# A decoder layer on one core: the maximum of the cross attention's scores runs 15 steps ahead of the scores instead of 17

## The reference, cut to what matters

```python
x = layernorm(x + linear_attention(x))              # 8 heads of 64
Q = (x @ Wq + bq)    # 16 heads of 16, 2048 queries
K, V = (ctx @ Wk + bk), (ctx @ Wv + bv)             # 1601 keys
attn = softmax(Q K^T / sqrt(16), axis=-1)
x = layernorm(x + (attn @ V) @ Wo + bo)
x = layernorm(x + moe(x))    # 16 experts, the best 4 of each token, and a shared one
```

## Time and profile before

| | us |
|---|---|
| runs | 1095.07, 1096.03, 1097.78 |
| median | 1096.03 |
| profiled execution | 1086.56 |
| its span | 1084.7 |
| mean granted TensorE clock | 0.940 of full speed |
| TensorE busy | 951.4 (88%) |
| VectorE busy | 732.9 (68%) |
| ScalarE busy | 648.0 (60%) |

### The profile page before, as it was taken

How to read it: one execution, slowest core, us unless ns; L and a number is a source line. 1 busy time by engine, 2 the same in 40 slices (tenths; PEclk the granted TensorE clock), 3 DMA queues, 4 the chain that set the end, 5 groups by cost and what they waited for, 6 DMA issues and landing times.

```text
span 1084.7 us, 19088 instructions
## 1 busy us (share of the span) xinstructions
PE 951.4 (88%) x6868; PEld 521.9 (48%) x6868; DVE 732.9 (68%) x1171; ACT 648.0 (60%) x1403; POOL 254.6 (23%) x306
## 2 busy tenths in 40 slices
PE   6997998779999999999999999998990698988890
PEld 2454566334444444444444444443340586776670
DVE  0206886798999998989989899889120343324773
ACT  1322223118888887878878788777870265654560
POOL 1006113600000000200002000000465255773654
PEclk9999999859999999999999999999895799999996
DMA  9007892200322112112211010011642246554763
GB/s 346 8 1 179 101 129 92 94 5 2 100 81 86 42 50 84 37 35 58 86 55 27 8 27 22 25 53 50 142 148 75 86 142 137 158 157 148 242 214 131
DMA packets 75800, 99.29 MB, mean 92 GB/s; under 512 B 17566, under 2 KB 58784, under 8 KB 75390
## 3 DMA queue, kind: packets, MB, share of 16 engines
q1 hardware_dynamic: 64252, 73.73, 26.8%
q0 software_dynamic: 7584, 20.79, 5.4%
q10 hardware_dynamic: 3872, 3.56, 1.0%
HBM read 52.45 MB, written 43.35 MB: 88 GB/s over the span
## 4 chain that ended last, share of the span: by engine, by line
PE 60%; DVE 17%; DMA 8%; issue 7%; POOL 6%; ACT 2%; SPq 0%; POOLq 0%; DVEq 0%; ACTq 0%
PE psum L1163 16%; PE psum L1053 13%; DVE mpart L1466 9%; PE psum L1149 7%; PE psum L1318 6%; POOL sorted_d L677 4%; PE psum L982 3%; PE psum L1336 3%; PE psum L1015 3%; DMA x_in<-sorted_d 2%; DMA given_d<-y_out,x_in 2%; PE psum L1279 2%; DMA sorted_d<-x_rows,slots 2%; PE psum L1103 1%; PE psum L1187 1%
## 5 line engine op out<-in xcount | busy, mean ns | idle before, releaser
L937 ACT ACTIVATE region<-psum 128x512 f32<-128x512 f32 (+1 forms) x832 | 448.6, 610 | 132.0 <-PE psum L1149 117.6
L1466 DVE TENSOR_REDUCE mpart<-psum 128x2 f32<-128x1024 f32 x384 | 461.7, 1222 | 39.4 <-PE psum L1053 36.4
L1163 PE MATMUL psum<-region 128*32 128x256 f32 (+1 forms) x3120 | 251.8, 395 | 7.4 <-ACT numT L852 7.4
L1053 PE MATMUL psum<-kstack,qstack 63*128 63x512 f32 (+1 forms) x1024 | 223.0, 463 | 19.9 <-DVE mpart L1466 19.5
L1053 PEld LDWEIGHTS psum<-kstack,qstack 63*128 63x128 f32 x1024 | 92.9, 194 | 194.0 <-issue 123.7
L1149 PE MATMUL psum<-qstack,kstack 64*128 64x512 f32 (+1 forms) x832 | 176.1, 412 | 0.1
L1683 DVE SCALAR_TENSOR_TENSOR silu_h<-tanh_h,psum 128x128 f32<-128x128 f32 x110 | 31.6, 287 | 150.7 <-ACT tanh_h L907 149.4
L1149 PEld LDWEIGHTS psum<-qstack,kstack 64*128 64x128 f32 (+1 forms) x832 | 111.3, 184 | 17.6 <-ACT region L937 14.5
L1163 PEld LDWEIGHTS psum<-region 128*32 128x32 f32 (+1 forms) x3120 | 62.2, 108 | 118.1 <-issue 75.7
L1318 PE MATMUL psum<-w_all,xT_in 128*128 x376 | 103.3, 399 | 3.8 <-issue 1.7
L685 POOL DMA_INDIRECT given_d<-y_out,x_in x94 | 93.4, 994 | 44.8 <-ACT y_out L921 27.3
(11 more groups left out here) (172 smaller groups left out, 937.5 us busy)
## 6 DMA issues: line engine op xcount, KB each, us to landing
x_in<-sorted_d SPq DMA_DIRECT2D x94, 129.0 KB, 2.5
sorted_d<-x_in SPq DMA_DIRECT2D x7, 1548.0 KB, 7.3
given<-given_d SPq DMA_DIRECT2D x16, 512.0 KB, 4.6
qstack<-qparts_d SPq DMA_DIRECT2D x96, 64.0 KB, 2.3
kstack<-kparts_d SPq DMA_DIRECT2D x6, 800.5 KB
qparts_d<-region SPq DMA_DIRECT2D x4, 1024.0 KB, 4.1
kparts_d<-region SPq DMA_DIRECT2D x4, 800.5 KB, 10.1
xT<-in_xT SPq DMA_DIRECT2D x1, 2048.0 KB, 9.2
```

Of the source, the lines that this page charges most:

```text
L937: act.activation(prob[0:rows_of, s % 3, j, :], ring(n)[0:rows_of], ACT.Exp).then_inc(ring_read, 1)
L1053: mm = pe.matmul(bank(unit_bank(u) + side)[:, at * w:(at + 1) * w], qstack[rows_of, buffer(G), p, t * P:(t + 1) * P], kstack[rows_of, g * ...
L1163: mm = pe.matmul(bank(NUM_BANK)[VW * j:VW * (j + 1), q], vals[0:r, g, kt, j, :], prob[0:r, s % 3, j, q], start=(kt == 0 and half == 0), st ...
L1466: dve.tensor_reduce(mpart[:, G % 2, qt, :, p, n], both, X, ALU.max).then_inc(max_read, 1)
```

## The change

LEAD falls from 17 to 15 steps, so that 30 units instead of 34 lie ahead of step 0 (24 instead of 28 in the lead-in loop), each group's last unit falls into kt = 10 instead of kt = 8, and all units are done after step 192 instead of 190. SP's stack_max moves from kt = 9 to kt = 11.

```diff
-LEAD = KT + 4
+LEAD = KT + 2
 FIRST_UNIT_AT = TILES + 7
 UNITS_IN_LOOP = TILES + 13 - FIRST_UNIT_AT
-STACK_MAX_AT = 9
+STACK_MAX_AT = 11
```

## The result

The changed kernel is slower. On another chip, where both are 12 to 13 us faster, twelve runs gave 1090.85 against 1083.97, ratio 1.0061 (1.0042 to 1.0080). The forecast was 1103.4.

What follows compares the result with a forecast made beforehand. Bound: TensorE and VectorE, without slack, until the slots are ready at step 188, then GpSimd's scatter. Lead-in -2.5, boundaries +8.9, clock +1, elsewhere 0 make +7.4 on 1096.03: 1103.4 us, range 1097.5 to 1109.

Steps and rivals of the forecast that it cites:

- Part 1: Lead-in: with four units fewer ahead, step 0's score loads start earlier, limited by group 0's maximum landing; gain 2.5 us.
- Part 2: Group boundaries: the maximum comes two steps later, its DMA chain outlasts the room, and TensorE stalls; loss 8.9 us.
- The eight plain boundaries: Into groups 1, 2, 3, 4, 6, 8, 10, 12: chain 5.5 us against room 4.6, so 0.9 us stall each.
- The five with longer steps: Into groups 5, 7, 9, 11, 13: out projection or gate work widens the room to 5.7 us; 0.25 us each.
- Part 3: TensorE's granted clock during the steps: between none and two more falls than before; +1 us, bounds -1.5 and +6.
- rival (b): TensorE's clock falls at most group boundaries, adding 12 us to the stalls, 1114.4 us in all; chance 0.08.
- Part 4: Last steps, SP's order, expert loads and scatter: moved work is covered or unwaited for; 0 us, bounds -6.7 and +3.
- finish_max passes some short gate operations on VectorE: VectorE's queue: finish_max moves past gate operations before which its reads are ordered anyway; cost 0.
- Nobody waits for them: SP's queue: loads issued ahead of the later maximum go out in what was a wait, with no waiter; cost 0.
- slots ready 6 to 8 us after 758.9: Sign of being right: VectorE has the slots of chunks 0 to 2 ready (step 188) that much later than before.
- (a): Boundary stalls cost nothing, as TensorE makes them up or the chain fits; 1093.5 or 1092.0 us; chance 0.07.
- (c): With later loads the first scatter lands in 2.6 us instead of 9.36, giving the loss back; 1096.7 us; chance 0.08.

Runs made afterwards that it cites:

- half the reads: The changed kernel with VectorE reading only the first 256 of each 512 scores; a read took 0.69 us instead of 1.22, a plain step still 2.47 us.
- the longer chains: The changed kernel with one or two more DMAs (copies of max_d) between the write's landing and the four reads; ratios to the kernel before 1.0182 and 1.0443.

## Why the prediction was right, point by point

**Part 1, the lead-in.** Forecast 2.5 us, measured 2.3 to 2.6 (237.3 and 236.8 against 239.6 and 239.4). The reason is shown: the first scores wait for the DMA, and with two reads instead of four they come 1.2 us earlier still.

**Part 2, the boundaries.** Forecast 8.9 us, measured 9.5 and 8.5. In the first profile two inner sizes were off, in ways that cancel. The eight plain boundaries cost 1.13 each instead of 0.95, the chain having a mean of 5.7 over these eight (5.3 to 6.1) where SP's mean wait had given 5.5. One mean hides two kinds: four chains with a quick landing and four with a slow one. The estimate by the Trainium skill had 1.3 for each of the eight.

The Trainium skill, "DMA: Bandwidth & Descriptors", section "Anatomy of one DMA", gives its 2.0 us for DMAs that GpSimd issues. Those here are issued by SyncE, and the quick landing of the write took 1.4 us, the slow ones 1.9 to 2.2.

The five with longer steps cost 0.09 instead of 0.25. Where each would and wouldn't wait was right at all fourteen. What the prediction had wrong is that nothing comes back: 0.12 us does in the step behind each stall, 1.2 in all. TensorE is at its own rate in a plain step, as half the reads show, but the first half step after a stall runs a little shorter.

**Part 3, the clock.** Forecast +1 us, and this step failed, harmlessly. No fall of the clock was added. In the first profile the one of before came again; after the start of the steps the clock rose sooner (the first three steps take 7.8 and 9.1 us in its two profiles, 9.4 and 10.1 in those of before), which gives 1.0 to 1.6 in these pairs. So the size was of the wrong sign here. That the change is the reason isn't shown: over all profiles these three steps take 8.3 to 10.1 at lead 17 and 7.1 to 9.2 at lead 15. The mechanism that the term stood for, rival (b), is real and begins just beyond this change: with the chain 0.6 us longer it is already half of what is lost on top.

**Part 4, elsewhere.** Forecast 0 with bounds of -6.7 and +3. The step that failed is "finish_max passes some short gate operations on VectorE", costed at 0. What is moved past the gate's work is not finish_max alone but the two short units ahead of it as well, and whole units that take their place cost 0.7 us in each of two groups, 1.4 in all; the other way round, step 0 of groups 8 and 12 (2.78 before) loses its delay behind the gate's work, 0.6 in all beyond the 0.12. The four units at the end and the last boundary's wait, though the last wait was up to 6.4 us and not 2, changed nothing that shows, and the stretch from slots to the first tile is 91.8 against 94.2 and 92.2 against 89.0. "Nobody waits for them" was wrong of the expert load that SP now issues ahead of the last maximum: the maximum's own write lands late, 4.1 and 6.4 us after its issue in the change's two profiles (1.9 before). It is covered.

**The sum.** In the first pair of profiles: -2.3 for the lead-in, -1.6 for the clock at the start, +9.5 for the stalls, -1.2 that comes back, +1.4 and -0.6 around the gate: 5.2, where the slots are 5.4 us later. In the second pair: -2.6 - 1.0 + 8.5 - 1.2 + 1.4 - 0.6 = 4.5, where they are 4.7 later. So the attention is accounted for; forecast were 7.4, and the sign "slots ready 6 to 8 us after 758.9" was missed from below, with 5.4 and 4.7. The medians differ by 8.6 and 6.9, the latter with an interval of 4.6 to 8.7 us. The 2 to 3 us between slots and median have no place in the profiles. The spread of runs without any change (1079.9 to 1089.3 on the second chip) could cover them, but that is not shown, and they stay open. That the median came within 1 us of 1103.4 is therefore in part luck: the attention gave 2 us less than was added up, and 2 to 3 us without a known place made up for it.

**The rivals.** (a) fell: the stalls are there and only an eighth of them is made up. (b) fell for this change and held for the longer chains. (c) fell: the first scatter's landing took 4.9 us instead of 9.36 in the changed kernel's profile, but another scatter then waited in its issue (7.7 us between 774.15 and 781.88), and the stretch as a whole was no shorter.

**A version that beats the kernel before** is not clear of the noise. Lead 15 or 16 with two reads has 0.9972 and 0.9979, each interval ending at 0.9998; they are 0.8 to 0.9% under the change, and 2 to 3 us under the kernel before.

## What to carry to other kernels

A lead counted in steps is really a room in time for one chain of transfers: measure that chain from its first releaser to its last landing, measure the room after the change, and compare the two at each place where it is waited for, not on average. If the chain is longer than the room, look first at what in it is issued one after another; here two DMAs fewer did what two more steps of lead had done. When work moves along an engine's queue, ask also which short instruction stood beside a long one and no longer does. Leave a margin for landings that take 2 to 3 us instead of 1.4, and for the clock: here stalls of up to 1.5 us cost only themselves, and most of those of 1.9 us and more also cost clock.

## What the runs showed of the hardware that was not expected

- The loss isn't linear in the stall. 7.3 us more of stalls, spread over a dozen places, cost 15.3 us, and 17.3 us more cost 43.0, while the granted clock fell to 0.50 for 6.8 to 10.2 us behind some of them, by the estimate above enough for the rest. Behind stalls of up to 1.5 us it stayed at 1.00, and behind two of 1.9.
- The write of the last group's negT took 4.1 to 10.3 us to land in all eight profiles with the maximum in SP's step 11, and 1.4 to 2.0 in the five others that record it. That 384 KB of weights had been issued on the same queue shortly before isn't enough: so they had in the others too, 3 to 11 us before. In the eight, their issue begins 2.5 to 3.6 us behind the slots, so once the scatter has begun; in the others at most 1.7 us behind them. This was not tried apart.
- Whether the write of negT lands in 1.4 or in 2 to 3 us goes with a single packet of the DMA queues of kind "instruction". Over groups 0 to 14 of the fourteen profiles 195 landings are recorded. In 81 of them such a packet (8 or 16 KB) starts between 0.3 us before the write's issue and 1.4 us after it: 75 of these took 1.8 us or more. Of the 114 others 109 took 1.4 to 1.5. This is a match in time; no run changed it by itself, so the cause isn't shown. A slow and a quick landing at lead 16, groups 3 and 4 (queues and issues in 331.5 to 334.9 and in 364.9 to 366.4):

```profile
q1 hardware_dynamic: 144, 0.02, 3.5%
q8 instruction: 1, 0.02, 1.6%
max_d<-negT SPq DMA_DIRECT2D x1, 16.0 KB, 3.3
```

```profile
q1 hardware_dynamic: 144, 0.02, 7.3%
max_d<-negT SPq DMA_DIRECT2D x1, 16.0 KB, 1.4
```

- After a stall of TensorE the next step was 2.35 us instead of 2.47 at every one of ten boundaries, and half the work of VectorE didn't change either number. What sets the 0.12 was not tried.
